# Attention and GRU kernel: products with V in 64x32 tiles ahead of the scores, V placed by three transfers

## What is computed

```python
x = x + attention(x, cond)      # per sequence: RMS norm, scale and shift from cond @ W_emb,
                                # qkv = xn @ W_qkv, 16 heads of 16, q and k RMS-normed per head,
                                # o = softmax(q k^T / 4) v ; o + o @ W_out
x = x + gru(cond, x)            # 32 steps, initial state cond:
                                # r, z = sigmoid(...), n = tanh(i_n + r * h_n), h = (1 - z) n + z h
```

## Time and profile before

| | us |
|---|---|
| median of 3 runs (340.23 to 343.07) | 342.57 |
| span of the profiled execution | 340.0 |
| PE busy | 323.3 (95%) |
| DVE busy | 246.3 (72%) |
| ACT busy | 238.0 (70%) |
| POOL busy | 224.5 (66%) |
| SP's issues of V strips, 124 of them | 34.0 KB each |

### The profile page before, as it was taken

One profiled execution on the slowest core, in us unless ns is written; L12 is line 12 of the kernel. 1 busy time (PEld: TensorE's weight loads), 2 busy tenths in 40 slices (PEclk: granted clock), 3 DMA queues, 4 the chain that ended last, 5 costly groups with the idle time before them and its releaser, 6 DMA issues.

```text
span 340.0 us, 12168 instructions
## 1 busy us (share of the span) xinstructions
PE 323.3 (95%) x4177; PEld 293.4 (86%) x4177; DVE 246.3 (72%) x665; ACT 238.0 (70%) x722; POOL 224.5 (66%) x404
## 2 busy tenths in 40 slices
PE   8988899899999999999986999999999999999994
PEld 8767788788888888888874999999999999999994
DVE  3778898888999999999996455565555556555555
ACT  4787777778888788889656566666666666666662
POOL 6787787867777877878778346555555555555542
PEclk9999999999999999999999999999999999999999
DMA  5965237742343333233332221111112111122221
GB/s 202 307 193 151 86 76 234 226 132 85 109 121 113 101 114 99 86 117 116 112 109 65 80 77 48 61 49 62 62 62 62 48 58 50 62 62 62 63 62 33
DMA packets 32205, 34.14 MB, mean 100 GB/s; under 512 B 5286, under 2 KB 26796, under 8 KB 32172
## 3 DMA queue, kind: packets, MB, share of 16 engines
q1 hardware_dynamic: 25868, 26.10, 25.6%
q10 hardware_dynamic: 6304, 7.61, 7.0%
HBM read 12.46 MB, written 8.39 MB: 61 GB/s over the span
## 4 chain that ended last, share of the span: by engine, by line
PE 78%; POOL 7%; SPq 4%; DMA 4%; issue 3%; DVE 3%; ACT 1%; POOLq 0%; DVEq 0%; ACTq 0%
PE bank L1287 38%; PE bank L1244 19%; PE bank L1400 4%; PE bank L1419 4%; PE bank L1388 4%; DMA operands<-operands 4%; PE bank L1531 3%; SPq L414 2%; POOL operands L485 2%; PE bank L1380 2%; SPq L405 2%; PE bank L1250 2%; PE bank L1371 2%; POOL xn L496 1%; POOL xn_lo L531 1%
## 5 line engine op out<-in xcount | busy, mean ns | idle before, releaser
L1287 PE MATMUL bank<-wih_lo,wo_parts 128*128 128x256 f32 x192 | 56.2, 294 | 0.0
L1287 PE MATMUL bank<-wih_hi,wo_parts 128*128 128x256 f32 x192 | 54.6, 285 | 0.2 <-POOL pair_lo L600 0.2
L1287 PE MATMUL bank<-wih_hi,pair_lo 128*128 128x256 f32 x192 | 52.8, 279 | 0.0
L1287 PE MATMUL bank<-wqkv_hi,hT_hi 128*128 128x256 f32 x192 | 52.5, 292 | 0.0
L611 POOL TENSOR_TENSOR operands<-operands,h 128x128 f32<-128x128 f32 x64 | 29.6, 462 | 34.2 <-ACT operands L932 33.4
L1287 PE MATMUL bank<-wqkv_lo,hT_hi 128*128 128x256 f32 x192 | 49.9, 279 | 0.0
L1187 DVE TENSOR_TENSOR operands<-bank,operands 128x128 f32<-128x128 f32 x64 | 18.6, 291 | 39.3 <-ACT operands L929 39.3
L1244 PE MATMUL bank<-wqkv_hi,xn_hi 128*128 128x512 f32 (+1 forms) x124 | 46.4, 375 | 0.2 <-POOL xn_lo L531 0.2
L618 POOL TENSOR_TENSOR w_emb_sb<-h,w_emb_sb 128x256 f32<-128x256 f32 x31 | 22.9, 737 | 30.7 <-DVE h L1204 30.7
L1287 PE MATMUL bank<-wqkv_hi,hT_lo 128*128 128x256 f32 x192 | 42.7, 279 | 0.0
L1244 PE MATMUL bank<-wqkv_hi,xn_lo 128*128 128x512 f32 (+1 forms) x124 | 41.9, 338 | 0.0
(11 more groups left out here) (138 smaller groups left out, 975.2 us busy)
## 6 DMA issues: line engine op xcount, KB each, us to landing
v_diag<-v_rows SPq DMA_DIRECT2D x124, 34.0 KB, 2.1
operands<-operands SPq DMA_DIRECT2D x32, 128.0 KB, 2.1
out_dram<-x ACTq DMA_DIRECT2D x16, 256.0 KB, 2.6
w_emb_sb<-out_dram SPq DMA_DIRECT2D x32, 128.0 KB, 2.1
operands<-operands SPq DMA_DIRECT2D x63, 64.0 KB, 2.0
out_dram<-w_emb_sb SPq DMA_DIRECT2D x31, 128.0 KB, 1.7
x_in<-in_x_dram SPq DMA_DIRECT2D x7, 512.0 KB, 8.6
stage_w<-in_L_cond_W_ih_dram ACTq DMA_DIRECT2D x2, 384.0 KB, 3.4
```

The source lines that it names most:

```text
L1287: return pe.matmul(dst, moved, gate_columns(weights, k, block), start=False, stop=True, skip_group_check=True)
```

## The change

Products with V are made in the scores' 64 x 32 tiles: for each head one product per half i of the partitions, 64 partitions of `probsT` against 2 x 17 columns of `v_diag`, so 32 products a group instead of 16, each with half the columns. They write to `o_tiles[i]`, 136 columns behind the scores in the scores' banks 3 and 4. `v_diag` has three strips a group instead of four: strip 1 holds sequences 1 and 2 (the two halves of the partitions read strips i and i+1), so V is placed by three transfers; for groups 3 and 4 ACT issues the last one. `p_v` gets a bank of its own (bank 5).

On PE a turn now is: V projection, result transposes, products with V of g, scores of g+1, and the rest as before. Result transposes no longer wait for the copy of V. DVE reads the outputs through one more dimension, and reciprocals also wait for the next group's scores, which write the same banks. The order of the last turns follows: the q and k transposes of the last group stand behind the scores, where those of other groups stand.

```diff
+VALUE_STRIPS = ((0, 1), (1, 2), (3, 1))
+OW = 2 * HEADS // 4 * VW
...
-        v_diag = sb("v_diag", [P, 4, GB, HEADS, VW])
+        v_diag = sb("v_diag", [P, 4, len(VALUE_STRIPS), HEADS, VW])
...
-        p_x2T, p_v = p_vx2[:, 0:D], p_vx2[:, D:2 * D]
+        p_x2T, p_v = p_x2zn[:, 0:D], p_vn[:, 0:D]
         s_tiles = [p_s[:, BANK * i:BANK * i + D] for i in range(2)]
+        o_tiles = [p_s[:, BANK * i + D:BANK * i + D + OW] for i in range(2)]
...
             def place_values(v, slot):
                 sp.wait_ge(v_ready, v + 1)
-                for b in range(2 if isinstance(v, int) and v in SHARED_VALUES else GB):
-                    rows = slice(T * b, T * b + T)
-                    sp.dma_start(v_diag[rows, slot, b, :, :].rearrange("p h f -> p (h f)"),
+                strips = VALUE_STRIPS[:-1] if isinstance(v, int) and v in SHARED_VALUES else VALUE_STRIPS
+                for i, (first, count) in enumerate(strips):
+                    rows = slice(T * first, T * (first + count))
+                    sp.dma_start(v_diag[rows, slot, i, :, :].rearrange("p h f -> p (h f)"),
...
             def reciprocals(o, slot):
                 dve.wait_ge(o_ps, o + 1)
-                dve.reciprocal(inv_sum[:, slot, :], o_heads[:, :, DH]).then_inc(inv_ready, 1)
+                dve.wait_ge(s_ps, capped(o, 2))
+                dve.reciprocal(inv_sum[:, slot, :].rearrange("p (i n) -> p i n", i=2), o_heads[:, :, :, DH])\
+                   .then_inc(inv_ready, 1)
...
             def result_transposes(d, slot):
                 pe.wait_ge(x2_ready, d + 1)
-                pe.wait_ge(v_ready, capped(d, PE_X2T - PE_V + (1 if isinstance(d, int) and d in LATE_RESULTS else 0)))
...
             def attention_products(g, slot, place):
                 pe.wait_ge(probsT_ready, g + 1)
-                pe.wait_ge(v_diag_ready[place], spread_by_four(g, place, GB))
+                pe.wait_ge(v_diag_ready[place], spread_by_four(g, place, len(VALUE_STRIPS)))
                 if later(g, 1):
                     pe.wait_ge(o_ready, g)
+                pe.sem_inc(outputs_clear, 1)
                 for hq in range(HEADS // 4):
                     for j in range(4):
...
-                        dst = p_o[32 * j:32 * j + 32, 0:GB * HEADS // 4 * VW]\
-                            .rearrange("p (b n f) -> p b n f", b=GB, f=VW)[:, :, hq, :]
-                        last = pe.matmul(dst, probsT[:, slot, column, :], v_diag[:, place, :, head, :],
-                                         start=True, stop=True)
+                        for i in range(2):
+                            rows = slice(2 * T * i, 2 * T * i + 2 * T)
+                            dst = o_tiles[i][32 * j:32 * j + 32, :].rearrange("p (n h f) -> p n h f", n=2, f=VW)[:, :, hq, :]
+                            last = pe.matmul(dst, probsT[rows, slot, column, :], v_diag[rows, place, i:i + 2, head, :],
+                                             start=True, stop=True)
                 last.then_inc(o_ps, 1)
...
-                if d is not None and not late_result:
-                    result_transposes(d, (u - PE_X2T) % 4)
                 g = group(base, u, PE_V)
                 if g is not None:
                     value_projection(g, (u - PE_V) % 2)
                 if turn_is(base, u, NG - 2 + PE_QKT):
                     query_key_transposes(NG - 2, (u - PE_QKT) % 2)
+                if d is not None and not late_result:
+                    result_transposes(d, (u - PE_X2T) % 4)
+                g = group(base, u, PE_PV)
+                if g is not None:
+                    attention_products(g, (u - PE_PV) % 2, (u - PE_PV) % 4)
                 g = group(base, u, PE_S)
                 if g is not None:
                     scores(g, (u - PE_S) % 2)
-                if turn_is(base, u, NG - 1 + PE_QKT):
-                    query_key_transposes(NG - 1, (u - PE_QKT) % 2)
-                g = group(base, u, PE_PV)
-                if g is not None:
-                    attention_products(g, (u - PE_PV) % 2, (u - PE_PV) % 4)
```

More of the change, by code:

```diff
@@ L162, in adaptive_attention_gru @@
         r_g, z_g, rh, npre, n_g, zh = (gru_tile(KC, P) for _ in range(6))
-        p_xTw, p_vx2, p_qkT = (bank(f"bank{i}") for i in range(3))
+        p_xTw, p_x2zn, p_qkT = (bank(f"bank{i}") for i in range(3))
         p_s = ctx.enter_context(nc.psum_tensor("bank3", [P, 2 * BANK], F32))
-        p_o = bank("bank5")
+        p_vn = bank("bank5")
         p_qk2 = ctx.enter_context(nc.psum_tensor("bank6", [P, 2 * BANK], F32))
@@ L243, in adaptive_attention_gru @@
         scores_clear = sem("scores_clear")
+        outputs_clear = sem("outputs_clear")
         square_x_free = sem("square_x_free")
@@ L336, in adaptive_attention_gru @@
         rz_banks = [p.rearrange("p (c f) -> p c f", c=KC)[:, :, 0:2 * P] for p in (p_qk2[:, :], p_s[:, :])]
-        n_banks = [p_qkT, p_o]
-        zn = p_vx2[:, D:2 * D].rearrange("p (c a) -> p c a", c=KC)
-        hT_banks = [p_xTw[:, 0:P], p_vx2[:, 0:P]]
+        n_banks = [p_qkT, p_vn]
+        zn = p_x2zn[:, D:2 * D].rearrange("p (c a) -> p c a", c=KC)
+        hT_banks = [p_xTw[:, 0:P], p_x2zn[:, 0:P]]
         def pair_index(base, n):
@@ L658, in _ @@
             act.wait_ge(vec_ps, 1)
[L659 removed]
+            act.copy(vec_cols[:, :], p_vn[:, 0:8]).then_inc(vec_cols_ready, 1)
             def shifts():
@@ L692, in load_gate_weights, with last_values_strip @@
                 act.dma_start(staged[:, i % KC, :], source[(i % KC) * P:(i % KC) * P + P, :]).then_inc(loaded[i % KC], 16)
-            def place_values(v, first, last):
+            def last_values_strip(v):
                 act.wait_ge(v_ready, v + 1)
-                for b in range(first, last):
-                    rows = slice(T * b, T * b + T)
-                    act.dma_start(v_diag[rows, v % 4, b, :, :].rearrange("p h f -> p (h f)"),
-                                  v_rows[rows, v % 4, :, :].rearrange("p h f -> p (h f)"))\
-                       .then_inc(v_diag_ready[v % 4], 16)
+                first, count = VALUE_STRIPS[-1]
+                rows, slot = slice(T * first, T * (first + count)), v % 4
+                act.dma_start(v_diag[rows, slot, len(VALUE_STRIPS) - 1, :, :].rearrange("p h f -> p (h f)"),
+                              v_rows[rows, slot, :, :].rearrange("p h f -> p (h f)"))\
+                   .then_inc(v_diag_ready[slot], 16)
             def last_keys():
@@ L899, in body @@
                     if turn_is(base, u, v + ACT_V):
-                        place_values(v, 2, GB)
+                        last_values_strip(v)
                 for i in range(4):
@@ L1359, in value_projection @@
                     pe.wait_ge(v_ready, g)
-                if isinstance(g, int) and g == NG - 1:
-                    pe.wait_ge(x2T_ready, LATE_RESULTS[0])
                 hi, lo = projection_input(slot)
@@ L1452, in body @@
                     scores(g, (u - PE_S) % 2)
-                if turn_is(base, u, NG - 1 + PE_QKT):
-                    query_key_transposes(NG - 1, (u - PE_QKT) % 2)
-                g = group(base, u, PE_PV)
-                if g is not None:
-                    attention_products(g, (u - PE_PV) % 2, (u - PE_PV) % 4)
                 g = group(base, u, PE_QKT)
-                if g is not None and not (isinstance(g, int) and g >= NG - 2):
+                if g is not None and not (isinstance(g, int) and g == NG - 2):
                     query_key_transposes(g, (u - PE_QKT) % 2)
@@ L1463, in body @@
                     pe.wait_ge(o_ready, NG)
+                    pe.wait_ge(v_ready, NG)
                     clear_gates(1).then_inc(gates_clear[1], 1)
```

10 lines of the change are left out of this document (5 added, 5 removed).

## The result

| | before | after |
|---|---|---|
| median, us | 342.54 | 346.98 (345.9 to 348.83) |
| ratio to before | | 1.0166, 95% interval 1.0129 to 1.0203 |
| span of the profiled execution, us | 340.0 | 347.0 |

The change made the kernel 4.4 us slower; 337.9 had been forecast. The profiled execution of after is the slowest of its four (348.83), so differences read from its trace are up to 2 us larger than those of the medians.

A forecast was written before the change was run, and what follows sets the result against it. PE was taken to bound the attention loop, with DVE next. Gains of 1.1 + 0.6 + 1.0 + 2.6 less 0.6 in the tail made 4.7 us, off 342.57 giving 337.9 us; range 334 to 342.

The forecast's parts named there:

- DVE as the next bound: Attention loop: DVE, busy 4.77 of 5.05 us a turn, has 0.28 us of room; rival that it takes over: 339.9, 27%.
- The rate of starts: Products with V: 64 records on eight tiles start every 0.0067 us, 0.43 us in all.
- The rival by count: TensorE's feed, not columns, sets 0.013 us a record, so 64 records cost 0.83 us: 347 us in all, 10%.
- The change of shape: PE's turn: three changes of array shape become two; products plus scores take 1.03 instead of 1.21 us, 0.18 less a turn.
- PE's sequencer: Rival of no effect: waiting for probsT, it eats the saved change of shape; nothing gained a turn, 341.5 us, 7%.
- (a): 35 to 55 us: products with V run inside the scores' wait for keys, 0.61, plus three turns at 0.17: 1.1 us gained.
- (b): 55 to 66 us: late keys hold the scores, and the products with V hide under that wait: 0.61 us gained.
- (c): 66.37 to 82.01 us: an excess of 0.5 goes as SP is relieved, plus three turns at 0.17: 1.0 us gained.
- SP's three transfers: Three V transfers for four: 0.6 us less issuing a turn, nothing in the steady turn, 0.5 gained from 66.37 to 82.01.
- The tail: 158 to 195 us: scores behind products waiting for probsT delay row_max, 2.1 in all; earlier last keys offset: net 0.6 lost.

The follow-up runs named there:

- half the products: The changed kernel with every second group of four heads left out of the products with V in all groups but the first: 336.16 us, ratio 0.982.
- PE kept busy: The changed kernel with 18 products that nobody reads ahead of the products with V in turn 36: 346.12 us, ratio 1.0094.
- waits ahead: The changed kernel with the scores' waits made before the products with V instead of between the two blocks: 347.66 us, ratio 1.0163.
- the older probsT: The changed kernel with the products with V of group g reading the probsT of g - 1: 345.29 us, ratio 1.0132.

## Why the prediction was wrong

**What bounds the kernel: right.** PE without idle time in the loop, before and after. DVE as the next bound, near 4.77: right too; half the products ran into it at 4.79.

**The rate of starts: the step that failed first.** The forecast took the spacing of the first eight records of a block, 0.0067 us, for all 64, hence 0.43 us. Measured: 0.165 us for the first 32 and 0.40 for the rest, a pause and then 0.017 a product, 0.57 in all. The spacing of a block's first records says how fast PE starts what is already queued; how fast the rest arrives must be read behind the first 32. The block of 32 records in the earlier trace rows couldn't show it, since it fits into that number. The rival by count had the mechanism ("a queue filled in advance may feed those eight") and 10%; its own rate, 0.013 a record throughout, gave 0.83 and was too high. That its total, 347, is what was measured is luck: it had some 5 us of loss in the turns, where 1.2 were found, and 0.6 in the tail.

**The change of shape: about right in size as far as the sum tells, and eaten.** Forecast: 0.43 + 0.40 + 0.19, written as 1.03 for the pair (the terms make 1.02). With the scores' waits out of the way it is 1.20: 0.14 of the difference is the rate, and 0.07 the scores' own starts, which the slow supply then reaches. No run isolates the change of shape. As changed the pair is 1.21 in one turn of four and 1.31 in the others: the scores' waits and the instructions around them take 0.10 more. That cost had no term in the sum. The prediction named "PE's sequencer" as a rival at 7%, but with no effect as its worst end. Per turn -0.17 became +0.08; over fifteen turns -2.6 became +1.2.

**The products hidden under waits for keys, (a) and (b): right in size.** Without the tiles' saving (a), (b) and (c) come to about 1.7. The two kernels with the new order in the early turns only are 1.8 and 1.5 us faster by their ratios. Of the changed kernel this can't be told so well: its scores of that turn come at 82.01, as before, so by PE's position it is 83.22 - (82.01 + 0.61) = 0.6 ahead, but the same program up to turn 36 is 0.2 behind in the execution with PE kept busy (82.79).

**SP's three transfers: not shown.** 0.5 had been put down. Four transfers instead of three made no difference that the medians can tell, and their waits for keys appear with three transfers too.

**The tail: the largest miss.** Right were the mechanism (row_max behind scores behind products behind probsT) and that the last scores no longer wait for a DMA. The size, -0.6, was wrong: the order alone from turn 34 on costs 1.0%, 3.6 us (1.5 to 5.7). Three terms failed. The step from probsT's end to row_max was put at 1.26. At the full clock it is 1.51 in the changed kernel, of which 186.84 - 185.47 = 1.37 lie between the products' start and row_max, where the sum had 0.43 + 0.67 + 0.10 = 1.20: the rate of starts again. With the old tiles it is 1.55 (176.40 + 0.71 = 177.11 to 178.66, in the run with the order from turn 34 on), and 2.10 where PE had stood still before it and ran at the lower clock. The sum had the clock at full speed throughout, as before; it had not asked what 1.9 and 2.4 us of standing still do to it. And the residual x comes later behind DVE: the wait for it (L1380, after L1385) is 2.2 us instead of 1.5, a term the sum did not have.

**The books**, for the profiled executions (forecast 335.3, measured 347.0): 2.1 us up to 82 (2.7 forecast, 0.6 had), 3.8 in the loop (-2.6, +1.2), 5.9 in the tail. There PE's position is 157.86 + 1.21 = 159.07 before and 159.06 + 0.61 = 159.67 after, 0.6 behind; at the GRU it is 7.1 behind, so 6.5 were lost where 0.6 was put. Together 11.8, against 11.7. Of the tail's 6.5 some 2.1 are there at the full clock too, by the execution with four transfers. The other 4.4 came with the lower clock and the pause of 1.23 us, not separated, and make this execution the slowest of its four. The order's 3.6 by its own runs have some of the lower clock in them as well.

## What to carry to other kernels

Smaller tiles cut columns but double the products, and past the first 16 fp32 products of a block PE here took one only every 17 ns, after a pause of 77 (25 ns on average): count products as well as columns, and read the rate behind the first 32 records. An order that hides work in the steady part can be a loss in the last turns, where the chain runs through two engines: try it on the turns where it pays and keep the old order in the others (0.9948 here). Ask of each new wait on PE what the work behind it costs at half the granted clock: most of the waits of 1.9 to 2.4 us here were followed by the fall, some were not. Before comparing positions in two traces, look at their granted clock, and at how far two executions of the same program lie apart (over 2 us at 82 us here).

## What the runs showed of the hardware

- Starts of fp32 records of 34 columns on different 64x32 tiles come every 5 ns for the first 32 of a block. Then comes a pause of 0.077 us, and a product of two records every 17 ns, at 34 and at 64 columns. The floor of about 25 ns between starts that the Trainium skill gives (TensorE: Matmul & The Clock Gate, "Wait — 56ns, not 53.3ns?") does not hold for products on different tiles in these traces.
- Two products in succession on one tile cost more than alternating ones: 0.97 us against 0.78 for the same 32 products of 64 columns.
- 2.37 us (changed kernel), 2.31 (waits ahead) and 1.86 (order from turn 34 on) of PE standing still were followed by a granted clock of 0.50 (1.2 GHz) for 3.4 to 6.8 us. Waits of 1.55 and 1.58 us in the kernel with the order up to turn 33, whose mean clock is 1.0, were not, nor were 2.32 us with four transfers and 2.17 with the order alone: the length of the wait alone does not decide.
- PE stood 1.23 us in the middle of four transposes in unrolled code, with nothing it waits for in the trace, and 1.54 us at the same place in the run with the older probsT. Two more variants of the changed kernel had pauses of 0.7 and 1.0 us called "issue" at L1319 or its counterpart. The cause is not shown, and what is lost by them varies between executions.
